# Gated layer of a four-layer graph network: the turns of two groups are made in a row, in two PSUM banks, in every second slot

## What is computed

```python
    def _L1_gnn_ref(input, in_matrix, out_matrix, w3_w, w3_b, u3_w, u3_b, w4_w, w4_b, w5_w, w5_b, u5_w, u5_b, time_step):
...
        def step(h, _):
            m_in = jnp.einsum('nm,bmd->bnd', in_matrix, h)
            m_out = jnp.einsum('nm,bmd->bnd', out_matrix, h)
            av = jnp.concatenate([m_in, m_out], axis=-1)
            u3 = h @ u3_w.T + u3_b
            z = jax.nn.sigmoid(av @ w3_w.T + w3_b + u3)
            r = jax.nn.sigmoid(av @ w4_w.T + w4_b + u3)
            hv = jnp.tanh(av @ w5_w.T + w5_b + (r * h @ u5_w.T + u5_b))
            h = (1.0 - z) * h + z * hv
            return (h, None)
...
    x = _layernorm(x + _L1_gnn_ref(x, adj, adj, L1_gnn_w3_w, L1_gnn_w3_b, L1_gnn_u3_w, L1_gnn_u3_b, L1_gnn_w4_w, L1_gnn_w4_b, L1_gnn_w5_w, L1_gnn_w5_b, L1_gnn_u5_w, L1_gnn_u5_b, 5), axis=-1)
```

## Time and profile before

| | us |
|---|---|
| median of 3 runs | 1386.44 |
| lowest and highest | 1385.45, 1387.39 |
| the profiled execution | 1387.39 |
| its span, first to last instruction | 1385.2 |
| PE busy in the span | 1349.8 |
| DVE, ACT, POOL busy | 1108.6, 927.9, 753.7 |

### The profile page before, as it was taken

How to read it: one execution, slowest core, us unless ns; L and a number is a source line. 1 busy time by engine, 2 the same in 40 slices (tenths; PEclk the granted TensorE clock), 3 DMA queues, 4 the chain that set the end, 5 groups by cost and what they waited for, 6 DMA issues and landing times.

```text
span 1385.2 us, 26908 instructions
## 1 busy us (share of the span) xinstructions
PE 1349.8 (97%) x8470; PEld 1184.3 (85%) x8470; DVE 1108.6 (80%) x2632; ACT 927.9 (67%) x1666; POOL 753.7 (54%) x745
## 2 busy tenths in 40 slices
PE   9999979999999999999999999999889999999995
PEld 7888868888888888888888888887689999999994
DVE  5888878777778777778777787777688888888885
ACT  5666647677777776777777777766546666666664
POOL 4111127666666666666666666665435555555553
PEclk9999999999999999999999999999999999999998
DMA  3222232000021000020000110000212222222211
GB/s 107 96 92 91 96 103 77 1 0 0 9 82 32 0 0 0 30 83 8 0 0 0 46 46 1 0 0 8 76 54 70 70 68 68 68 68 68 68 39 38
DMA packets 60041, 61.16 MB, mean 44 GB/s; under 512 B 4691, under 2 KB 39381, under 8 KB 59989
## 3 DMA queue, kind: packets, MB, share of 16 engines
q1 hardware_dynamic: 59556, 60.31, 13.6%
q10 hardware_dynamic: 432, 0.20, 0.1%
HBM read 35.33 MB, written 25.17 MB: 44 GB/s over the span
## 4 chain that ended last, share of the span: by engine, by line
PE 94%; DVE 3%; ACT 2%; issue 1%; POOL 0%; ACTq 0%; POOLq 0%; DVEq 0%
PE psum L969 6%; PE psum L663 5%; PE psum L665 5%; PE psum L651 5%; PE psum L346 4%; PE psum L365 4%; PE psum L981 3%; PE psum L983 3%; PE psum L706 3%; PE psum L695 3%; PE psum L678 3%; PE psum L707 3%; PE psum L676 3%; PE psum L696 3%; PE psum L699 3%; PE psum L698 3%
## 5 line engine op out<-in xcount | busy, mean ns | idle before, releaser
L626 POOL TENSOR_TENSOR rh_lo<-rh,rh_hi 128x512 fp32r<-128x512 f32 x160 | 207.1, 1294 | 265.6 <-ACT rh_hi L741 265.6
L632 POOL TENSOR_TENSOR h_lo<-h,h_hi 128x512 fp32r<-128x512 f32 x160 | 216.6, 1354 | 12.8
L741 ACT CAST rh_hi<-rh 128x512 fp32r<-128x512 f32 x160 | 99.4, 621 | 149.2 <-DVE rh L773 149.2
L754 DVE TENSOR_TENSOR psum<-psum,h 128x512 f32<-128x512 f32 x160 | 111.9, 699 | 103.5 <-ACT psum L745 103.5
L663 PE MATMUL psum<-adj_t_hi,hn_hi 128*128 128x256 f32 x640 | 172.1, 303 | 1.0 <-DVE m_lo L767 1.0
L738 ACT ACTIVATE psum<-psum,bias_cols 128x512 f32<-128x512 f32 x160 | 106.8, 667 | 80.1 <-PE psum L683 80.0
L665 PE MATMUL psum<-adj_t_hi,hn_lo 128*128 128x256 f32 x640 | 158.9, 282 | 0.0
L773 DVE TENSOR_TENSOR rh<-psum,h 128x512 f32<-128x512 f32 x160 | 110.1, 688 | 50.3 <-ACT psum L738 50.2
L663 PEld LDWEIGHTS psum<-adj_t_hi,hn_hi 128*128 128x128 f32 x640 | 121.8, 190 | 1.9 <-issue 1.8
L665 PEld LDWEIGHTS psum<-adj_t_hi,hn_lo 128*128 128x128 f32 x640 | 122.2, 191 | 0.0
L728 ACT ACTIVATE z<-psum,bias_cols 128x512 f32<-128x512 f32 x160 | 111.3, 695 | 0.0
(11 more groups left out here) (184 smaller groups left out, 4119.8 us busy)
## 6 DMA issues: line engine op xcount, KB each, us to landing
x_in<-in_x_dram SPq DMA_DIRECT2D x32, 256.0 KB, 2.8
x_dram<-x SPq DMA_DIRECT2D x32, 256.0 KB, 2.1
g_x<-x_dram SPq DMA_DIRECT2D x32, 256.0 KB, 3.3
h_dram<-h SPq DMA_DIRECT2D x32, 256.0 KB, 2.0
ht<-h_dram SPq DMA_DIRECT2D x32, 256.0 KB, 2.9
c_x<-x_dram SPq DMA_DIRECT2D x32, 256.0 KB, 3.1
out_dram<-res SPq DMA_DIRECT2D x32, 256.0 KB, 2.4
conv_in<-in_L_gnn_weight_dram SPq DMA_DIRECT2D x1, 448.0 KB, 4.8
```

Source lines behind the costliest of these rows:

```text
L626: pool.tensor_tensor(rh_lo[:, q, :], rh[:, q, :], rh_hi[:, q, :].bitcast(F32), ALU.subtract).then_inc(rh_lo_done, 1)
L632: pool.tensor_tensor(h_lo[:, q, :], h[:, (g - 1) % G, :], h_hi[:, q, :].bitcast(F32), ALU.subtract).then_inc(h_lo_done, 1)
L754: dve.tensor_tensor(cb, cb, hg, ALU.subtract).then_inc(dif_done, 1)
```

## The change

Where `paired` holds (slots 8 to 151), an even slot makes the turns of its own group and of the next one, one after the other, and an odd slot makes none. The even group is turned into bank 0, the odd one into bank 7 (`B_HN_ODD`), and ScalarE and VectorE read the bank that belongs to the group. A turn waits for the low half of the last group in its own bank only: s - 1 instead of s, except for the first group of a step, which keeps s. The code of the turn stands in a function of its own. The first transposes of the convolution wait for the last paired group's low half, since they write bank 7.

```diff
-    B_HN, B_M, B_R, B_GATE = 0, 1, 2, 4
+    B_HN, B_M, B_R, B_GATE, B_HN_ODD = 0, 1, 2, 4, 7
...
+    def paired(base, g):
+
+        return not isinstance(base, int) or G <= base + g < SLOTS - G
+
+    def hn_bank(base, g):
+        return B_HN_ODD if paired(base, g) and g % 2 else B_HN
...
     def tensor(pe):
+        def turn(base, g, k, bank):
+
+            s = base + g
+            if k is not None:
+                pe.wait_ge(x1_loaded[g], k * 16 + 16)
+            else:
+                pe.wait_ge(h_done, s - G + 1)
+
+            wait_count(pe, hn_lo_done, s - 1 if paired(base, g) and g > 0 else s)
+            if isinstance(base, int) and s == 0:
+                pe.wait_ge(earlier["xt_done"], GROUPS)
+            for i in range(TILES):
+                src = x1[:, g, i, :] if k is not None else h[:, g, i * 128:(i + 1) * 128]
+                mm = pe.transpose(psum[:, bank, i * 128:(i + 1) * 128], src, ident[:, :])
+            mm.then_inc(hn_mm, 1)
+
         def slot(base, g, k):
             s = base + g
-            if live(base, g, 0):
...
-                wait_count(pe, hn_lo_done, s)
...
-                    mm = pe.transpose(psum[:, B_HN, i * 128:(i + 1) * 128], src, ident[:, :])
-                mm.then_inc(hn_mm, 1)
+            if not paired(base, g):
+                if live(base, g, 0):
+                    turn(base, g, k, B_HN)
+            elif g % 2 == 0:
+                turn(base, g, k, B_HN)
+                turn(base, g + 1, k, B_HN_ODD)
...
-                    act.copy(h[:, g, :], psum[:, B_HN, :])
+                    act.copy(h[:, g, :], psum[:, hn_bank(base, g), :])
...
-                    act.copy(hn_hi[:, g % 2, :, :].rearrange("p i d -> p (i d)"), psum[:, B_HN, :]).then_inc(hn_hi_done, 1)
+                    act.copy(hn_hi[:, g % 2, :, :].rearrange("p i d -> p (i d)"), psum[:, hn_bank(base, g), :]).then_inc(hn_hi_done, 1)
...
-                src = x1[:, g, :, :].rearrange("p i d -> p (i d)") if k is not None else psum[:, B_HN, :]
+                src = x1[:, g, :, :].rearrange("p i d -> p (i d)") if k is not None else psum[:, hn_bank(base, g), :]
...
                 wait_count(pe, y1_done, s)
+                if isinstance(it, int) and s == 0:
+                    pe.wait_ge(earlier["hn_lo_done"], earlier["pairs_end"])
```

More of the change, by code:

```diff
@@ L781, in gated_layer @@
     sems = {"h_out": h_out, "hn_lo_done": hn_lo_done, "m_lo_done": m_lo_done, "z_done": z_done,
-            "rh_done": rh_done, "h_done": h_done, "slots": SLOTS}
+            "rh_done": rh_done, "h_done": h_done, "slots": SLOTS, "pairs_end": SLOTS - G}
     return programs, (earlier, sems)
```

## The result

The changed kernel takes 1380.59 us (median of 6 runs, 1379.07 to 1381.38), the kernel before 1386.03 us in the same comparison (6 runs). The ratio is 0.9958, with a 95% interval of 0.9947 to 0.9969: faster by 0.4%, 4.3 to 7.3 us. The range (1380.5 to 1389.0) just holds the time.

A forecast was written before the change was run, and what follows sets the result against it. TensorE was taken as full in steady slots, a ScalarE and VectorE loop as the bound in x1 slots. Savings of 0.3 + 0.3 = 0.6 us from the median 1386.44 gave 1385.8 us, range 1380.5 to 1389.0.

The forecast's parts named there:

- What bounds the kernel: Gated layer: TensorE is full in steady slots; in slots reading x1, ScalarE and VectorE set the pace, 5.08 us.
- The turn's borders, 0.3 us: Steady slots: 72 fewer ways into and out of turns save between 0 and 0.7 us; 0.3 taken.
- The rival that took the 0.08 us of the first L663 for a cost: First matmul after a turn: the exit really costs 0.08 us, so 5.8 us go, giving 1380.6; chance 0.11.
- The sign named for it: Profile after: two slots together lasting 9.64 us or less, instead of the forecast 9.72, would show the turn's exit cost.
- a pace that could change: TensorE's matmul spacing shifts by 0.04 us per pair: 1382.9 if it falls (chance 0.11), 1388.7 if it rises (0.07).
- The moved waits: Even slots run 0.44 us later behind the turns; idle time covers it, VectorE keeping 0.01: priced at nothing.
- x1 slots, 0.3 us: Three stretches reading x1: only each stretch's last wait can go, saving between 0 and 1.2 us; 0.3 taken.
- The clock: Rival: TensorE's granted clock in the layer falls below 1.00, making the kernel slower; chance 0.02.

The follow-up runs named there:

- the last run: Changed kernel, but in x1 slots of sets 1 to 3 ScalarE makes the high half before copying the bank into h: 1375.58 us, ratio to before 0.9918.
- split_turns: Changed kernel, but an even slot's second turn stands behind the aggregation instead of behind the first turn: 1381.01 us, ratio to before 0.9963.

## Why the prediction was wrong, step by step

- **What bounds the kernel**: right. In h slots TensorE's own row of matmuls: from 640 to 780 us it is busy for 140.00 of 140.00 us before and after, at a granted clock of 1.00, and no wait of that stretch is TensorE's, before or after; in x1 slots the loop over ScalarE and VectorE, which the last run opened.
- **The turn's borders, 0.3 us**: right that they cost next to nothing. The reading of the starts and ends held: with twice as many borders the pair still took 9.62 to 9.64 us. The rival that took the 0.08 us of the first L663 for a cost gave the right sum for a wrong reason, by luck: its 72 x 0.08 = 5.8 counts 12 pairs of x1 slots, in which TensorE waits anyway, while the h slots lost 60 x 0.12 = 7.2. The sign named for it, a pair of 9.64 us or less, came true as well and could not tell it from the pace; the 0.20 us from the first L679 to the L681 are still there, and it was split_turns that told them apart.
- **The step that failed** is a term missing from the sum: whatever stands behind the turns was priced at nothing, without a reason. I took the spacing of the other 23 matmuls of a slot as given, and it changed; that is 0.12 us a pair, 7.2 us, against the 0.6 of the whole sum. The earlier trace rows already had two slots with the same instructions, 4.84 and 4.88 us, and I named a pace that could change as a rival, with one step of 0.04 us per pair and 0.11 as its chance. What came was three such steps, 0.12, because both slots of a pair went over: 1380.6 instead of 1382.9. Before, one slot in two and three 512-column matmuls of the other stood at the slower pace. Had I worked out the whole way, instead of one step, the rival would have come near: nine matmuls in 2.10 or 2.06 us are 0.0044 each, 18 of them in a pair 0.08, in 60 pairs 4.8 us, 1381.6. Nothing in the rows would have said that it comes, though.
- **The moved waits**: right in h slots. Idle time before r's sigmoid (the new L754) is 0.79 us in even and 0.19 in odd slots (0.7 and 0.25 foreseen), and VectorE has none left before r*h in odd slots, as was foreseen; from 640 to 780 us no wait of TensorE came of it:

```profile
644.07 0.66 ACT L754 ACTIVATE psum<-psum,bias_cols 128x512 f32<-128x512 f32 x1 [0.79 <-PE psum L699]
...
648.43 0.66 ACT L754 ACTIVATE psum<-psum,bias_cols 128x512 f32<-128x512 f32 x1 [0.19 <-PE psum L699]
...
649.13 0.69 DVE L789 TENSOR_TENSOR rh<-psum,h 128x512 f32<-128x512 f32 x1
```

- **x1 slots, 0.3 us**: not borne out. Eight slots from 403.72 to 443.82 us before are 40.10 us, and after, from 402.42 to 442.41, 39.99; in the other two sets the stretch grew, by 0.14 us (599.34 to 639.15, and 596.14 to 636.09) and by 0.23 (794.67 to 834.40, and 789.69 to 829.65). The loop keeps its 5.08 us, so the quicker TensorE only waits longer for it: from 402 to 447 us 1.8 us before, and now 2.4, of which 1.0 stands at the candidate (L711), for GpSimd's low half. Three such stretches have no share in the gain.
- **The clock**: did not fall. With eight transposes in a row in two banks (8 x 0.11 = 0.88 us) the granted clock of the stretch is 1.00, as it was with four in one bank. What a lower clock costs stands in the same trace of before: from 209 to 210 us the granted clock is 0.50, and a 512-column matmul takes 0.43 us there instead of 0.23.

What stays open is what in TensorE's row picks the pace. Single turns ahead of the aggregation give the mixture; pairs, single turns behind the aggregation, the split pair, and one small matmul more ahead of a single turn (32 or 64 columns) all give the quicker pace nearly throughout. The banks, the waits, GpSimd, and ten of the twelve operations of ScalarE and VectorE have been ruled out, each by a run, and the filler gets the quicker pace with one bank and the old waits. The supply of instructions to TensorE and the two operations that were not cut have not been tested. That the moment at which the matmuls begin behind the turn decides is my guess; no run sets that moment by itself.

## What to carry to other kernels

When an engine is full, its instructions can still have more than one spacing, as TensorE's do here (0.229 and 0.233 us): compare the same line in two slots of the trace, work out what the slower spacing costs over the whole stage, and treat a rearrangement as a draw between the spacings even where each instruction's price says zero. Then test the cause apart from the edit: here the pairing itself is not what pays, and a split pair gains as much. And look for the few slots that another loop bounds; a swap of two copies there was worth nearly as much as the whole change.

## What was not expected of the hardware

- fp32r matmuls of 512 columns at a granted clock of 1.00 stand 0.233 or 0.229 us apart (2.10 and 2.06 us for nine), those of 256 columns between 0.11 and 0.12, without a wait in either case, and in the kernel before the pattern of the two repeats every two slots (4.84 and 4.88 us). In the gated layer of the twelve traces nine of the 512-column ones never take less than 2.05 us, 0.228 each.
- A 32-column fp32 matmul ahead of the transposes costs 0.17 us where one of the transposes (128 columns) costs 0.11, and one of 64 columns leaves the slot as long (4.97 us). It stands in the trace as two instructions (256 for 128 fillers), a transpose as one.
- VectorE's subtraction with both inputs in SBUF took 951 ns on average in the kernel before and 806 with GpSimd's work cut down. In six x1 slots of set 1 the medians are 1004 and 692 (400 to 440 us, GpSimd busy for 27.5 and 6.9 of the 40 us). The same with one input in PSUM took 681 on average in both. GpSimd's busy time alone does not set it: with single turns behind the aggregation, GpSimd is busy for 27.2 us of that stretch and the median is 717.
